# One order of steps for each engine in a fused gate network, in place of one order for all

## What is computed

```python
xn = _layernorm(x)
s = attn(xn)          # 16 heads of 16, heads mixed before and after the softmax
g = silu(ffn(xn))     # 2 layers of local attention (8 heads of 64) and a gated FFN
return x + s * g

# attn:
logits = einsum('bhid,bhjd->bhij', rope(q), rope(k)) * SCALE
logits = einsum('bhij,gh->bgij', logits, Wpre)
attn = einsum('bhij,gh->bgij', softmax(logits), Wpost)
out = einsum('bhij,bhjd->bhid', attn, v) @ Wout.T + bout

# one layer of ffn (windows of 128 tokens that see themselves and the window before):
h = shift_token(x); q, k, v = split(h @ wqkv); q, k = xpos(l2norm(q) * qs, l2norm(k) * ks)
x = x + local_attention(q, k, v) @ wo
h = layernorm(shift_token(x)) * lg + lb
a, g = split(h @ w1 + b1); x = x + (a * gelu(g)) @ w2 + b2
```

## Time and profile before

| | us |
|---|---|
| median of three runs | 5149.01 (5140.02 to 5149.17) |
| the profiled execution | 5135.53 |
| its span, first to last instruction | 5133.6 |

### The profile page before, as it was taken

One profiled execution on the slowest core, in us unless ns is written; L12 is line 12 of the kernel. 1 busy time (PEld: TensorE's weight loads), 2 busy tenths in 40 slices (PEclk: granted clock), 3 DMA queues, 4 the chain that ended last, 5 costly groups with the idle time before them and its releaser, 6 DMA issues. The chain is left out here.

```text
span 5133.6 us, 181222 instructions
## 1 busy us (share of the span) xinstructions
PE 5019.6 (98%) x74904; PEld 4094.3 (80%) x74904; DVE 3367.3 (66%) x8313; ACT 2914.6 (57%) x7589; POOL 2610.9 (51%) x2308
## 2 busy tenths in 40 slices
PE   6999999999999999999999999999999999999998
PEld 5887888878888788887887878888887888878787
DVE  6557676666766567666676666766667676676765
ACT  4556555565655566555655556555565555565554
POOL 5446554455645456454464544645546455464543
PEclk9999999999999999999999999999999999999999
DMA  2211112121111211112111111201111012111110
GB/s 83 99 70 54 60 36 68 47 66 48 40 63 47 69 45 40 64 54 65 42 63 40 63 55 43 71 32 63 55 54 60 32 63 68 41 60 56 40 51 18
DMA packets 51408, 281.07 MB, mean 55 GB/s; under 512 B 5280, under 2 KB 22688, under 8 KB 33696
## 3 DMA queue, kind: packets, MB, share of 16 engines
q1 hardware_dynamic: 39840, 252.69, 13.5%
q0 software_dynamic: 10752, 16.78, 1.8%
HBM read 249.01 MB, written 28.84 MB: 54 GB/s over the span
## 5 line engine op out<-in xcount | busy, mean ns | idle before, releaser
L1501 POOL TENSOR_TENSOR q_lo<-q_mix,q_hi 128x512 fp32r<-128x512 f32 x512 | 672.0, 1313 | 1367.6 <-ACT q_hi L985 1367.5
L998 ACT ACTIVATE probs<-bank_S,neg_max 128x512 f32<-128x512 f32 x1024 | 699.3, 684 | 796.7 <-DVE neg_max L1231 640.8
L1231 DVE TENSOR_REDUCE neg_max<-bank_S 128x1 f32<-128x512 f32 x1024 | 694.9, 686 | 363.4 <-PE bank_S L715 361.1
L713 PE MATMUL bank_S<-k_hi,q_lo 128*128 128x512 f32 x2048 | 872.0, 426 | 7.5 <-POOL q_lo L1501 5.5
L715 PE MATMUL bank_S<-k_hi,q_hi 128*128 128x512 f32 x2048 | 804.4, 393 | 0.2 <-issue 0.2
L714 PE MATMUL bank_S<-k_lo,q_hi 128*128 128x512 f32 x2048 | 804.3, 393 | 0.0
L730 PEld LDWEIGHTS bank_M<-mixer_n,probs 64*64 64x64 f32 x32768 | 530.2, 135 | 171.9 <-issue 148.5
L1496 POOL TENSOR_TENSOR q_mix<-q_rope,w_pre 128x256 f32<-128x256 f32 x1024 | 634.2, 647 | 45.3 <-POOL q_lo L1501 0.9
L730 PE MATMUL bank_M<-mixer_n,probs 64*64 64x64 f32 x32768 | 597.0, 221 | 18.8 <-DVE att L1291 14.5
L1527 POOL TENSOR_TENSOR l_probs<-l_probs,l_inv 128x1024 f32<-128x1024 f32 (+1 forms) x256 | 436.9, 1707 | 223.8 <-DVE l_inv L1334 222.0
L1057 ACT ACTIVATE l_probs<-l_probs,l_least 128x256 f32<-128x256 f32 (+1 forms) x1024 | 480.0, 472 | 85.4 <-DVE l_least L1314 83.3
(11 more groups left out here) (142 smaller groups left out, 10085.7 us busy)
## 6 DMA issues: line engine op xcount, KB each, us to landing
w_qkv_hi<-split_qkv SPq DMA_DIRECT2D x30, 1536.0 KB, 6.7
w_qkv_lo<-split_qkv SPq DMA_DIRECT2D x30, 1536.0 KB, 6.3
w_hi<-split SPq DMA_DIRECT2D x30, 1408.0 KB, 6.1
w_lo<-split SPq DMA_DIRECT2D x30, 1408.0 KB, 8.5
w<-in_w SPq DMA_DIRECT2D x32, 768.0 KB, 4.2
w_o<-in_w_o SPq DMA_DIRECT2D x32, 512.0 KB, 5.1
x_in<-in_x POOLq DMA_DIRECT2D x16, 512.0 KB, 4.5
out_y<-in_x SPq DMA_DIRECT2D x16, 512.0 KB, 7.7
```

What stands on the lines that cost most here:

```text
L713: mm(bank[k][:], q_lo[q], k_hi[:, s, :], start=(s == 0), stop=False)
L998: fn(probs[:, n % PB, :], bank[k][:], ACT.Exp, bias=neg_max[:, n % 2:n % 2 + 1], accum_out=row_sum[:, n % 4:n % 4 + 1]).then_inc(emptied[k ...
L1231: v.tensor_reduce(neg_max[:, n % 2:n % 2 + 1], bank[k][:], AX.X, ALU.max, negate=True)\
L1501: g.tensor_tensor(q_lo[:, c % QB], q_mix[:], q_hi[:, c % QB].bitcast(F32), ALU.subtract)\
```

## The change

`ORDER` goes. In its place stand five tables, `SP_ORDER`, `PE_ORDER`, `ACT_ORDER`, `DVE_ORDER` and `POOL_ORDER`; each names the steps that its engine has work in. `program()` takes the name of an engine and reads that engine's table for batches 1 to 14; the numbers of the bank fillings come from PE's. `FIRST_ORDER` and `LAST_ORDER` stay and are still common to all engines. No instruction is added or taken away, and no wait is: the functions of the steps are untouched. Set against the part of `ORDER` that an engine used to read, its own table has another step at 95 of 219 places on PE, 156 of 237 on ACT, 179 of 265 on DVE, 58 of 105 on POOL and 11 of 86 on SP.

```diff
-ORDER = """
-expand.0 part.0 expand.1 part.1 qkv.0.0 join.0.0 scores.0 expand.2 scores.1 qkv.0.1 mixers.0 k_turn.0.0 part.2 bound
...
-expand.6 sigmoid.0 mix.2 mixers.3 q_turn.0.3 part.6 scores.8 scores.9 k_turn.0.3 expand.7 sigmoid.1 mix.3 part.7
...
-local_values.0.6 p_turn.0.7 scores.22 local_values.0.7 mixers.10 scores.23 part.13 mix.10 mixers.11 out_proj.0.3
-half_turn.0 mix.11 shift_turn.0 scores.24 scores.25 project.0 expand.14 part.14 values.2 mixers.12 h_scale.0 scores.26
...
-scores.31 scores.32 expand.18 part.18 expand.19 qkv.1.0 mixers.15 join.1.0 scores.33 scores.34 part.19 mix.15
-q_turn.1.0 mixers.16 qkv.1.1 expand.20 k_turn.1.0 join.1.1 qkv.1.2 values.3 q_turn.1.1 part.20 k_turn.1.1 scores.35
...
-out_proj.1.3 expand.30 project.2 half_turn.1 scores.56 part.30 expand.31 shift_turn.1 mix.27 scores.57 scores.58
...
+PE_ORDER = """
+qkv.0.0 scores.0 scores.1 qkv.0.1 k_turn.0.0 scores.2 scores.3 mix.0 q_turn.0.0 qkv.0.2 k_turn.0.1 q_turn.0.1 scores.4
+scores.5 mix.1 qkv.0.3 q_turn.0.2 scores.6 k_turn.0.2 scores.7 mix.2 scores.8 q_turn.0.3 k_turn.0.3 scores.9 mix.3
...
+local_values.0.7 scores.23 mix.10 out_proj.0.3 scores.24 half_turn.0 mix.11 shift_turn.0 scores.25 project.0 scores.26
+values.2 scores.27 h_turn.0 mix.12 scores.28 up.0.0 mix.13 up.0.1 up.0.2 up.0.3 up.0.4 up.0.5 scores.29 scores.30
+down.0.0 down.0.1 down.0.2 down.0.3 mix.14 x_turn.1 scores.31 scores.32 qkv.1.0 qkv.1.1 mix.15 q_turn.1.0 scores.33
+scores.34 k_turn.1.0 qkv.1.2 values.3 k_turn.1.1 scores.35 mix.16 q_turn.1.1 qkv.1.3 scores.36 q_turn.1.2 k_turn.1.2
...
+local_values.1.5 p_turn.1.6 project.2 scores.52 scores.53 mix.25 out_proj.1.2 local_values.1.6 p_turn.1.7 scores.54
+local_values.1.7 scores.55 mix.26 out_proj.1.3 scores.56 half_turn.1 mix.27 shift_turn.1 scores.57 scores.58 values.6
...
+ACT_ORDER = """
+part.0 part.1 qkv.0.0 bound scores.0 scores.1 qkv.0.1 part.2 mixers.0 scores.2 scores.3 part.3 mix.0 q_turn.0.0
...
+scores.30 mixers.14 part.16 part.17 mix.14 x_turn.1 part.18 scores.31 mixers.15 scores.32 qkv.1.0 qkv.1.1 q_turn.1.0
+part.19 scores.33 mixers.16 mix.15 qkv.1.2 values.3 part.20 scores.34 scores.35 mixers.17 q_turn.1.1 mix.16 qkv.1.3
...
+DVE_ORDER = """
+bound qkv.0.0 join.0.0 scores.0 scores.1 qkv.0.1 mixers.0 k_turn.0.0 sigmoid.0 scores.2 scores.3 join.0.1 mix.0
...
+mixers.14 down.0.0 down.0.1 down.0.2 mix.13 down.0.3 mix.14 x_turn.1 scores.31 scores.32 mixers.15 qkv.1.0 join.1.0
+qkv.1.1 mix.15 scores.33 scores.34 k_turn.1.0 mixers.16 join.1.1 qkv.1.2 k_turn.1.1 scores.35 mix.16 join.1.2
...
+POOL_ORDER = """
+expand.0 part.0 expand.1 qkv.0.0 join.0.0 part.1 expand.2 qkv.0.1 part.2 expand.3 join.0.1 part.3 expand.4 part.4
+expand.5 qkv.0.2 join.0.2 part.5 qkv.0.3 join.0.3 expand.6 part.6 expand.7 part.7 weigh.0.0 expand.8 weigh.0.1 part.8
...
-def step_order():
-    return steps_in(ORDER)
+def step_order(engine="PE"):
+    return steps_in({"SP": SP_ORDER, "PE": PE_ORDER, "ACT": ACT_ORDER, "DVE": DVE_ORDER, "POOL": POOL_ORDER}[engine])
...
-def program():
+def program(engine="PE"):
...
-        steps += [(step, b + (step in AHEAD)) for step in (step_order() if b else first_order()) if b or step not in BEHIND]
+        steps += [(step, b + (step in AHEAD)) for step in (step_order(engine) if b else first_order()) if b or step not in BEHIND]
...
-            def run(self, eng, steps):
-
+            def run(self, name, eng, steps):
+
+                steps_of_all = program(name)
                 for step, b in steps_of_all:
```

More of the change, by code:

```diff
@@ L131 @@
[L131 to L135, removed]
@@ L146 @@
[L146 to L150, removed]
@@ new lines @@
+up.1.4 values.7 x_turn.0 project.3 up.1.5 talk_k talk_q talk_v down.1.0 down.1.1 down.1.2 down.1.3
+"""
+ACT_ORDER = """
+part.0 part.1 qkv.0.0 bound scores.0 scores.1 qkv.0.1 part.2 mixers.0 scores.2 scores.3 part.3 mix.0 q_turn.0.0
+mixers.1 qkv.0.2 part.4 scores.4 scores.5 mixers.2 q_turn.0.1 part.5 mix.1 qkv.0.3 scores.6 q_turn.0.2 mix.2 scores.7
+q_turn.0.3 mixers.3 part.6 scores.8 scores.9 mix.3 local_scores.0.0 part.7 scores.10 mixers.4 values.0
+local_scores.0.1 part.8 scores.11 scores.12 p_turn.0.0 mixers.5 mix.4 local_scores.0.2 scores.13 p_turn.0.1 scores.14
@@ new lines @@
+up.1.2 mix.31 up.1.3 up.1.4 values.7 x_turn.0 up.1.5 talk_k talk_q
+"""
+DVE_ORDER = """
+bound qkv.0.0 join.0.0 scores.0 scores.1 qkv.0.1 mixers.0 k_turn.0.0 sigmoid.0 scores.2 scores.3 join.0.1 mix.0
+mixers.1 qkv.0.2 k_turn.0.1 scores.4 scores.5 join.0.2 mixers.2 mix.1 qkv.0.3 k_turn.0.2 scores.6 join.0.3 scores.7
+mix.2 scores.8 mixers.3 k_turn.0.3 sigmoid.1 scores.9 local_scores.0.0 mix.3 scores.10 scores.11 weigh.0.0 mixers.4
+local_scores.0.1 sigmoid.2 scores.12 weigh.0.1 p_turn.0.0 mix.4 mixers.5 local_scores.0.2 scores.13 mix.5 scores.14
@@ new lines @@
+out_proj.1.1 local_scores.1.7 p_turn.1.5 mix.24 scores.50 scores.51 mixers.25 local_values.1.5 weigh.1.7 p_turn.1.6
+project.2 mix.25 scores.52 scores.53 out_proj.1.2 mixers.26 p_turn.1.7 local_values.1.6 scores.54 local_values.1.7
+scores.55 mix.26 out_proj.1.3 mixers.27 scores.56 mix.27 shift_turn.1 scores.57 scores.58 mixers.28 h_scale.1
+scores.59 mix.28 mixers.29 scores.60 h_turn.1 mix.29 scores.61 mixers.30 norm up.1.0 up.1.1 scores.62 scores.63
+mixers.31 mix.30 up.1.2 mix.31 up.1.3 scale up.1.4 x_turn.0 up.1.5 talk_k project.3 talk_v down.1.0 down.1.1 down.1.2
@@ L1122, in _ @@
             }
-            now.run(act, steps)
+            now.run("ACT", act, steps)
         @block.vector
@@ L1444, in _ @@
             }
-            now.run(dve, steps)
+            now.run("DVE", dve, steps)
         @block.gpsimd
@@ L1560, in _ @@
             }
-            now.run(pool, steps)
+            now.run("POOL", pool, steps)
 def shape_constants():
```

80 lines of the change are left out of this document (61 added, 19 removed).

## The result

Twelve runs of the changed kernel have a median of 5151.84 us (5141.99 to 5161.39), twelve of the kernel before beside them 5142.68 us. The ratio is 1.0018, with a 95% interval of [1.0011, 1.0025]. The change makes the kernel 0.1 to 0.25% slower, where 5114 us had been forecast. The profiled execution took 5154.01 us, against 5135.53 before, and its span is 5152.1 us.

What follows compares the result with a forecast made beforehand. It took PE's dense feeding as the bound; per batch -3.2 - 0.6 + 0.9 + 0.6 = -2.3, about -2.5 us with some idle time going, -35 us for 14 batches: 5149 to 5114 us, range 5065 to 5155.

Steps and rivals of the forecast that it cites:

- The bound: Batches 1 to 14: how densely PE is fed sets the end; PE is visibly idle 3.7 us a batch.
- Four waits removed: PE's waits for DVE at mix.3, values.2, half_turn.0 and half_turn.1, each pair parted by a scores step: minus 3.2 us a batch.
- mix.3's term: mix.3 straight behind k_turn.0.3 waits for DVE to empty bank M1; scores.9 between them saves 1.1 us, 14 times.
- POOL's part.1: part.1 moves behind join.0.0 on POOL, so PE's scores.2 newly waits: plus 0.9 us a batch, lower end 0.
- Thin distances: Five or six places where PE barely gets DVE's or ACT's results in time: plus 0.6 us a batch, ends 0 and 3.
- Other neighbours and remainder: PE's other new neighbouring steps, minus 0.6 us a batch, and some remaining idle time going, taking -2.3 to about -2.5.
- next door: Rival: PE's waits only shift to the next bank fillings, no change: 5142 to 5156, about 5149; chance 0.14.
- Two qkv steps in a row: Rival: qkv.1.1 behind qkv.1.0 makes DVE and ACT late at scores.35 or scores.36, +3 us a batch: 5191; chance 0.13.
- Everything goes: Rival: the remaining idle time closes too, no new wait comes, 6 us a batch: 5065; chance 0.13.
- Much faster: Rival: PE's weight-load row, 80% busy, shows the room; a third of the way to that floor gives 4863; chance 0.02.

Runs made afterwards that it cites:

- a_store: Changed kernel with only store moved in POOL_ORDER, from before weigh.0.4 to behind weigh.0.5: 5133.66 us, ratio 0.9981 to the kernel before.
- a_best_mix3: a_psj with scores.19 and scores.43 moved behind values.1 and values.4 on PE, and mix.3 put back right behind k_turn.0.3: 5153.51 us, 21.7 slower than without the latter.
- a_pool: Changed kernel with only part.1 put back before qkv.0.0 in POOL_ORDER: 5145.40 us, ratio 1.0006 to the kernel before.
- a_psj: Changed kernel with three POOL_ORDER moves: store behind weigh.0.5, part.1 back before qkv.0.0, join.1.1 before expand.20: 5112.99 us, ratio 0.9950 to the kernel before.
- b_store: Kernel before with only store moved earlier in ORDER, from behind p_turn.0.4 to before weigh.0.4: 5153.33 us, ratio 1.0025 to the kernel before.
- a_spread: a_psj with scores.18, mix.20 and scores.49 moved in PE_ORDER, scores.49 also on ACT and DVE: 5145.90 us, ratio 1.001 to the kernel before.

## Why the prediction was wrong

- **The bound.** That PE's feed sets the end was right. But I listed the 3.7 us of idle time a batch under waits that come back at the same step, and took the remainder for small change that would shrink with them ("with some part of PE's remaining idle time (3.7 less what is named) going too"). That was the step that failed. Of the 52.5 us of idle time, the three rows are 30.8. The kernel before already has 24.5 us in 21 gaps at the packets' edges, rows with "issue" as releaser, and these have a cause of their own. With the change they grow to 56.5; the moved store is shown as a cause of more than half of the growth (a_store: 37.0), a denser order is argued for the rest.
- **Four waits removed, -3.2 us a batch.** Right: the four places give back 3.2 us from start to start, and mix.3's term, 1.1 us, came out at 1.12, 1.34 with its neighbours, when it was put back (a_best_mix3). The others were not put back one by one.
- **POOL's part.1, +0.9.** Right in place and size: scores.2 starts 0.82 us late in every batch, 14 times, and a_pool takes 10.8 us of 11.5 out of the repeated part.
- **Thin distances, +0.6, ends 0 and 3.** Right in size by luck, since it came from elsewhere. k_turn.1.1 behind values.3 waits 0.60 us in 13 of the 14 batches for POOL's join.1.1, at a place that I hadn't named; I put it down to qkv.1.1 standing straight behind qkv.1.0, which I had followed through DVE and ACT but not through POOL; a_psj, with join.1.1 1.2 us earlier on POOL, is without it.
- **Other neighbours and remainder.** The repeated part came out at -1.5 us a batch, not -2.3 to -2.5. By the steps, the four waits (-3.2), part.1 (+0.82) and k_turn.1.1 (+0.60) leave +0.3 for everything else, where the sum had -0.6 for the neighbours and about -0.2 for idle time going too. So the neighbours' term had the wrong sign; which of them cost this I didn't isolate.
- **POOL's table, the store.** Missing from the working altogether. I costed part.1 and went through bound, sigmoid and the copies, but store moved, too: it issues a transfer, which now begins eight of PE's steps earlier, at local_values.0.2 and not at out_proj.0.1. a_store and b_store price its new place at 11.6 to 18.2 us.
- **The clock.** Not in the working either. The trace before has one fall behind a long gap; five after the change cost some 6 us more than that one.
- **The range.** 5151.84 us lies within the stated 5065 to 5155, but at its slow end, which had been taken in for "next door". That mechanism didn't happen, so this is luck.
- **The rivals.** Two qkv steps in a row: no wait of its kind came. Next door: not for the four waits. Its form, no change in the end, is near the outcome, but its mechanism is not what happened. Everything goes: without the store's and POOL's errors the kernel is at 5113, near the forecast, and far from 5065. I don't count this as the forecast being right, since it took three moves to get there. Much faster: PE's weight loads stay at 80% of the span in the changed kernel, and no order tried has a median under 5112 us.

Ledger from the kernel before to the one after, in the profiled executions: -20.7 repeated part; gaps under the store +19.9, under the load of x_in -7.9, under loads of weights +8.4, under none +12.5, together +32.9; smaller irregular delays +6.1, nearly all of it the lower clock; +18.3 in all.

**What stays open.** That loads of weights make the gaps beside which they stand (+8.4 us) isn't shown; no run moved such a load. In 7 of the 11 the trace speaks against the load as the whole reason: there the packet started 3.4 to 9.9 us after PE entered the one before it, while the load began only 3.6 us or more after that moment, or had ended 1.9 us or more before the packet started. The load of x_in (-7.9 us), which no run moved either, had ended 1.7 to 2.4 us before the packet started in all four of its gaps. The +12.5 us under none I put down to density: a_spread has 15 us less of this kind, but a slower PE with it, and no run names the moves that brought them in. Several packets of this kind start 2 to 4 us late with nothing beside them. What makes a packet start so late, other than the store, stays open. Nor was it tried to give single engines the new tables and leave the others the old one, since the tables depend on each other.
